# Routers with a place for every step's rows, three sets of moments, earlier masks, and an identity matrix that TensorE turns between its work

## The reference, cut to what matters

```python
x = x + 0.5 * _L0_ffn_ref(_layernorm(x), gate_w, w_gate, w_up, w_down)   # first router
x = x + _L0_attn_ref(_layernorm(x), ...)
x = x + 0.5 * _L0_ffn_ref(_layernorm(x), gate_w, w_gate, w_up, w_down)   # second router
...
# inside _L0_ffn_ref: T = 4096 tokens, E = 64 experts, K = 8, C = 128 places in an expert
logits = x2 @ gate_w.T
probs = softmax(logits)
top_w, top_i = top_k(probs, K)
pos = cumulative count of the token within its expert, over tokens in order
valid = pos < C
xg[e, pos] = x2[tok]                  # the experts' inputs
```

## Time and profile before

| | |
|---|---|
| median of 3 runs | 2716.4 us (2715.36 to 2718.21) |
| the profiled execution, its own time | 2715.87 us |
| its span in the profile | 2714.1 us |
| first router, from the first load to the table | about 7 to 105 us of the span |
| second router | about 1845 to 1944 us |
| mean granted clock of PE over the span | 0.948 |

### The profile page before, as it was taken

The page is one execution under the profiler, slowest core; times in us unless marked ns, Lnnn a source line. Parts: engine busy times, 40 slices in busy tenths (PEclk is TensorE's granted clock), DMA queues, the critical chain, the costliest instruction groups (busy, mean ns, idle before and its releaser), DMA issues. The chain is left out here.

```text
span 2714.1 us, 44233 instructions
## 1 busy us (share of the span) xinstructions
PE 2382.4 (88%) x16926; PEld 2110.7 (78%) x16926; DVE 1797.5 (66%) x3578; ACT 864.8 (32%) x1704; POOL 1239.9 (46%) x1214
## 2 busy tenths in 40 slices
PE   6556589999999999999999999986566488999998
PEld 6444479999999999999999999976454377888887
DVE  5433268888888888888888888865422256677654
ACT  4322233333333333333333333323322132333332
POOL 3378634555455455545554555452278622122111
PEclk9988799999999999999999999995599888999999
DMA  6999600000000000000000000004599710000000
GB/s 205 308 225 223 142 12 7 19 16 21 5 19 18 20 5 17 20 21 5 17 21 20 5 17 20 13 3 134 151 244 216 150 39 24 24 24 24 8 16 16
DMA packets 196928, 169.51 MB, mean 62 GB/s; under 512 B 28944, under 2 KB 189680, under 8 KB 196208
## 3 DMA queue, kind: packets, MB, share of 16 engines
q1 hardware_dynamic: 168144, 123.94, 15.5%
q0 software_dynamic: 24576, 37.77, 7.6%
q10 hardware_dynamic: 4000, 4.98, 0.6%
HBM read 117.94 MB, written 53.13 MB: 63 GB/s over the span
## 5 line engine op out<-in xcount | busy, mean ns | idle before, releaser
L971 POOL TENSOR_TENSOR a_orstd<-a_ms,minus_half 128x8 f32<-128x8 f32 x64 | 106.7, 1667 | 494.0 <-DVE a_ms L1131 494.0
L951 POOL TENSOR_SCALAR a_pick<-a_index,lut_row 128x258 f32<-128x258 int32 x240 | 280.7, 1170 | 24.3
L1124 DVE RECIPROCAL a_rz<-a_rz 128x256 f32<-128x256 f32 x128 | 215.5, 1715 | 0.0
L779 DVE TENSOR_TENSOR e_hT<-e_psH,e_sil 128x128 f32<-128x128 f32 x128 | 37.3, 291 | 259.6 <-ACT e_sil L737 259.6
L663 PE MATMUL e_psX<-ident,e_xg 128*128 128x128 f32 x256 | 61.6, 327 | 163.0 <-DMA e_xg<-rows,slot_tok 162.5
L663 PEld LDWEIGHTS e_psX<-ident,e_xg 128*128 128x128 f32 x256 | 30.6, 155 | 209.5 <-DMA e_xg<-rows,slot_tok 206.8
L1333 PEld LDWEIGHTS a_psD<-a_v,a_at 128*128 128x128 f32 x1536 | 181.3, 192 | 7.1 <-issue 1.4
L954 POOL TENSOR_TENSOR a_found<-a_found,a_pick 128x258 f32<-128x258 f32 x240 | 177.2, 738 | 20.0
L1333 PE MATMUL a_psD<-a_v,a_at 128*128 128x128 f32 x1536 | 181.9, 275 | 1.2 <-DVE a_at L1104 1.2
L633 POOL DMA_INDIRECT e_xg<-rows,slot_tok x128 | 127.4, 995 | 104.6 <-POOLq L252 66.2
L1104 DVE TENSOR_TENSOR a_at<-a_psB,causal 128x384 f32<-128x384 f32 x256 | 130.1, 550 | 49.2 <-PE a_psB L1270 49.2
(11 more groups left out here) (261 smaller groups left out, 7706.9 us busy)
## 6 DMA issues: line engine op xcount, KB each, us to landing
e_wg<-in_L_ffn_w_gate SPq DMA_DIRECT2D x128, 128.0 KB, 3.4
e_wu<-in_L_ffn_w_up SPq DMA_DIRECT2D x128, 128.0 KB, 3.7
e_wd<-in_L_ffn_w_down SPq DMA_DIRECT2D x128, 128.0 KB, 4.3
rows<-r_row SPq DMA_DIRECT2D x32, 320.0 KB, 3.2
stream_b<-r_zeros SPq DMA_DIRECT2D x11, 384.0 KB
stream_c<-rows SPq DMA_DIRECT2D x33, 128.0 KB, 3.3
r_xt<-in_L_attn_hidden_states SPq DMA_DIRECT2D x16, 256.0 KB, 3.8
stream_a<-r_xt SPq DMA_DIRECT2D x16, 256.0 KB, 4.4
```

The costliest lines, as they stand in the source:

```text
L951: nc.gpsimd.tensor_scalar(pick[:, :, :], index[:, :, :], float(c), w["lut"][:, c:c + 1], ALU.is_equal, ALU.mult).then_inc(picked, 1)
L971: nc.gpsimd.tensor_tensor(out=flat(orstd[:, :, :]), in0=ms[:, :], in1=cst["minus_half"][:, 0:TT * HQ], op=ALU.pow).then_inc(orstd_ok, 1)
L1124: nc.vector.reciprocal(rz[:, a, :], rz[:, a, :]).then_inc(rz_ok, 1)
```

## The change

What it does:

- `xt` and `row` get one place for each of the 8 steps. All loads are issued at the start, none waits, and `normalise` no longer waits for a written row. In the first router `keep` stands in the loop at every step.
- Moments, scale and shift get 3 places (S) in place of 2, and `moments_of` and `scales` run three steps ahead in place of two.
- On PE the masks of step j stand ahead of the scores of step j+1.
- PE transposes the identity matrix into a PSUM bank of its own, `psF`, that nobody reads (`occupy(n)`): 30 times ahead of the first turn and 10 behind it, and in a step 4 times behind the masks, 4 behind the scores and 12 behind the turn. The last two steps have fewer, so that a router has 172 in all.

```diff
-    R = 4
     NP = 4
+    S = 3
...
-        xt = mem.sb("xt", [P, R, 2, 2, D])
-        row = mem.sb("row", [P, R, 2, 2, ROW])
-        bs = mem.sb("bs", [P, 2, 4, 6])
+        xt = mem.sb("xt", [P, NJ, 2, 2, D])
+        row = mem.sb("row", [P, NJ, 2, 2, ROW])
+        bs = mem.sb("bs", [P, S, 4, 6])
...
+        psF = mem.ps("psF", [P, P])
...
                 def load(j):
-                    if j >= R:
-                        for u in range(2):
-                            sp.wait_ge(normed[u], 2 * (j - R) + 2)
-                        if fresh:
-                            sp.wait_ge(x_kept[j % R], 32 * (j // R))
                     for u in range(2):
-                        sp.dma_start(xt[:, j % R, u, :, :], xv[2 * j + u]).then_inc(x_here[j % R], 16)
+                        sp.dma_start(xt[:, j, u, :, :], xv[2 * j + u]).then_inc(x_here[j], 16)
...
-                for j in range(1, R):
+                for j in range(1, NJ):
                     load(j)
...
                 for j in range(NJ):
-                    if fresh and j < NJ - R:
+                    if fresh:
                         keep(j)
                     rows_written(j)
-                    if j + R < NJ:
-                        load(j + R)
...
-                    for j in range(NJ - R, NJ):
-                        keep(j)
...
                 def normalise(j):
                     act.wait_ge(shift_ok, j + 1)
-                    if j >= R:
-                        act.wait_ge(row_out[j % R], 32 * (j // R))
...
-                scales(0)
-                scales(1)
+                for j in range(S):
+                    scales(j)
                 for j in range(NJ):
-                    if j + 2 < NJ:
-                        scales(j + 2)
+                    if j + S < NJ:
+                        scales(j + S)
                     weigh(j)
...
-                moments_of(0)
-                moments_of(1)
+                for j in range(S):
+                    moments_of(j)
                 for j in range(NJ):
                     choose(j)
-                    if j + 2 < NJ:
-                        moments_of(j + 2)
+                    if j + S < NJ:
+                        moments_of(j + S)
...
+                def occupy(n):
+
+                    for k in range(n):
+                        nc.tensor.transpose(psF[:, :], cst["ident"][:, :], cst["ident"][:, :])
+
...
+                occupy(30)
                 turn(0)
+                occupy(10)
                 pe.wait_ge(gw_ready, 1)
                 score(0)
                 turn(1)
                 for j in range(NJ):
-                    if j + 1 < NJ:
-                        score(j + 1)
                     for u in range(2):
                         pe.wait_ge(chosen_ok[u], j + 1)
...
                                             cst["ident"][:, :]).then_inc(maskT[u], 1)
+                    if j + 1 < NJ:
+                        occupy(4)
+                        score(j + 1)
+                    occupy(4)
                     if j + 2 < NJ:
                         turn(j + 2)
+                        occupy(12)
```

More of the change, by code:

```diff
@@ L160, in moe_router @@
         zeros = mem.sb("zeros", [P, (NTOK // P + 1) * D // NZ]) if fresh else None
-        xt = mem.sb("xt", [P, R, 2, 2, D])
-        row = mem.sb("row", [P, R, 2, 2, ROW])
-        bs = mem.sb("bs", [P, 2, 4, 6])
[L164 to L168, removed]
+        xt = mem.sb("xt", [P, NJ, 2, 2, D])
+        row = mem.sb("row", [P, NJ, 2, 2, ROW])
+        bs = mem.sb("bs", [P, S, 4, 6])
+        mv = mem.sb("mv", [P, S, 4, 2])
+        ve = mem.sb("ve", [P, S, 4])
+        mean = mem.sb("mean", [P, S, 4])
+        rstd = mem.sb("rstd", [P, S, 4])
+        shift = mem.sb("shift", [P, S, 4])
         lnT = mem.sb("lnT", [P, 2, DC, 2 * P])
@@ L193, in moe_router @@
         psG = mem.ps("psG", [P, DC, E])
+        psF = mem.ps("psF", [P, P])
         gw_here, gw_turned, gw_ready = mem.sem("gw_here"), mem.sem("gw_turned"), mem.sem("gw_ready")
         zero_set, zero_out = mem.sem("zero_set"), mem.sem("zero_out")
-        x_here, x_kept, row_out = ([mem.sem(f"{n}{k}") for k in range(R)] for n in ("x_here", "x_kept", "row_out"))
+        x_here, x_kept, row_out = [mem.sem(f"x_here{k}") for k in range(NJ)], mem.sem("x_kept"), mem.sem("row_out")
         stats, moments, shifted, rstd_ok, shift_ok = (mem.sem(n) for n in ("stats", "moments", "shifted", "rstd_ok", "shift_ok"))
@@ L298, in _ @@
                         sp.dma_start(zv[:, k, :], zeros[:, :]).then_inc(zero_out, 16)
-                    for j in range(NJ - R, NJ):
-                        keep(j)
                     for raw, src, here in behind:
                         sp.dma_start(raw, src).then_inc(here, 16)
-                    for k in range(R):
-                        sp.wait_ge(x_kept[k], 32 * (NJ // R))
+                    sp.wait_ge(x_kept, 32 * NJ)
                     sp.wait_ge(zero_out, 16 * NZ + 32)
-                for k in range(R):
-                    sp.wait_ge(row_out[k], 32 * (NJ // R))
+                sp.wait_ge(row_out, 32 * NJ)
             @block.scalar
@@ L312, in normalise @@
                     act.wait_ge(shift_ok, j + 1)
-                    if j >= R:
-                        act.wait_ge(row_out[j % R], 32 * (j // R))
                     for u in range(2):
                         for h in range(2):
-                            nc.scalar.activation(row[:, j % R, u, h, 0:D], xt[:, j % R, u, h, :], ACT.Identity,
-                                                 bias=shift[:, j % 2, 2 * u + h:2 * u + h + 1],
-                                                 scale=rstd[:, j % 2, 2 * u + h:2 * u + h + 1]).then_inc(normed[u], 1)
+                            nc.scalar.activation(row[:, j, u, h, 0:D], xt[:, j, u, h, :], ACT.Identity,
+                                                 bias=shift[:, j % S, 2 * u + h:2 * u + h + 1],
+                                                 scale=rstd[:, j % S, 2 * u + h:2 * u + h + 1]).then_inc(normed[u], 1)
                 def turned_out(j):
@@ L382, in weigh @@
                     pool.wait_ge(rden_ok, j + 1)
-                    nc.gpsimd.tensor_tensor(out=row[:, j % R, :, :, :].rearrange("p u h c -> p (u h) c")[:, :, D:ROW], in0=ex[:, j % 2, :, :],
+                    nc.gpsimd.tensor_tensor(out=row[:, j, :, :, :].rearrange("p u h c -> p (u h) c")[:, :, D:ROW], in0=ex[:, j % 2, :, :],
                                             in1=rden[:, j % 2, :].unsqueeze(2).to_broadcast([P, 4, E]), op=ALU.mult).then_inc(weights, 1)
-                scales(0)
-                scales(1)
+                for j in range(S):
+                    scales(j)
                 for j in range(NJ):
-                    if j + 2 < NJ:
-                        scales(j + 2)
+                    if j + S < NJ:
+                        scales(j + S)
                     weigh(j)
@@ L497, in turn @@
                             for c in range(DC):
-                                nc.tensor.transpose(psT[u][:, c, h * P:(h + 1) * P], row[:, j % R, u, h, c * P:(c + 1) * P],
+                                nc.tensor.transpose(psT[u][:, c, h * P:(h + 1) * P], row[:, j, u, h, c * P:(c + 1) * P],
                                                     cst["ident"][:, :]).then_inc(turned[u], 1)
```

22 lines of the change are left out of this document (11 added, 11 removed).

## The result

| | before | after |
|---|---|---|
| median of 4 runs each | 2715.88 us (2710.7 to 2718.21) | 2699.64 us (2697.55 to 2703.7) |
| the profiled execution, own time / span | 2715.87 / 2714.1 us | 2703.7 / 2702.0 us |

The ratio is 0.9946, with a 95% interval of 0.9934 to 0.9957: 16.2 us less between the medians.

What follows compares the result with a forecast made beforehand. It took a ring of waits through PE, DVE, POOL and ACT at clock 0.50 to bound the routers, 6.96 us a step. 2 x (9.2 - 0.5) - 1.5 = 15.9 us less gave 2700.5 us, range 2694 to 2705.

Steps and rivals of the forecast that it cites:

- the sum: Whole kernel: 2 x (9.2 - 0.5) - 1.5 = 15.9 us less, giving 2700.5 us as the median.
- DVE sets the step: Router steps at clock 1.00: DVE's 5.6 us is longest; second to eighth choice takes 32.6 us in place of 41.77.
- choices farther apart than 5.6 us at a clock of 1.00: Router steps: a stated sign of being wrong; choices were expected 5.6 us apart.
- Does the clock rise?: Start of each router: PE's clock rises from 0.50 to 1.00 in the first 48 transposes and stays there.
- The masks ahead, the moments a step sooner. Both cut the ring.: Router steps: both reorderings leave a shorter ring, 5.1 us at clock 1.00 or 7.4 us at 0.50.
- the ring: Router loop of choice, moments, scales, normalising, turn, scores, masks, scans; two rounds make two steps, 41.77 us from second to eighth choice.
- The waits removed from `load` and `normalise` give nothing by themselves.: Router steps: no gain from removing these waits, as ACT waited for POOL's shift, not for a written row.
- The start: Each router up to its second choice: +0.5 us, with bounds of -2.0 to +1.1 us.
- The first router's DMA: First router's last counts: nearly full DMA could make them queue, +1.5 us, with bounds of 0 to about 10 us.
- The clock stays at 0.50: Rival, both routers: transposes don't raise the clock, a step takes 10.0 us, total about 2765 us; chance 0.18.
- The first router's queue: Rival: queued counts or traffic cost 6 to 10 us more, or the clock sometimes falls; 2705 to 2712 us; chance 0.14.
- No change: Rival: clock rises late, near the middle of each loop, so slow and fast steps cancel; 2711 to 2722 us; chance 0.05.

## Why the prediction was right, point by point

**The time.** Forecast 2700.5, measured 2699.64 us. Part of that exactness is luck: the routers of the profiled pair gave 11.1 us where the sum had 15.9, and its own time was 2703.7 where the forecast had 2700.0. The other three executions lie 2.7 to 6.2 us lower, and no trace shows where. The sign and the size of the main term are shown; the last 4 us are not.

**"DVE sets the step", 4 x 5.6 + 2 x 5.1 = 32.6 us.** Right in size: 32.9. It is made of four steps of 5.78 and two of 4.8 and 5.0. The 5.6 was DVE's work at 5.39 (too high by 0.2) without the 0.39 us beside POOL's L371, which the earlier trace rows could not show, as L371 and L404 did not meet there. One of the prediction's own signs of being wrong, choices farther apart than 5.6 us at a clock of 1.00, thus came true by this 0.2 us; it says that the size of DVE's step was off, not that another engine set it.

**"Does the clock rise?"** It rose among the first 30 transposes and stayed, as taken. With that the Trainium skill's rule, "TensorE: Matmul & The Clock Gate", "Part 4: PE-mode transpose", does not hold for these: nothing but transposes of 128 x 128 in fp32 ran on PE from 12.83 to 18.2 us and from 1844.56 to 1847.8 us, and the granted clock went from 0.50 to 1.00. (The durations beside the page's rule are for bf16.) "The step on which the sign hangs" holds only for a kernel with identities in it. The gain as a whole does not need the clock: places and moments alone give 0.9941, at a mean clock of 0.63 from 1858 to 1890 us.

**"The masks ahead, the moments a step sooner. Both cut the ring."** Half of this step failed. The moments cut it: taken back, the ring is 41 us again. The masks ahead don't: taken back, it is 0.5 us shorter, and the last choice another 0.65 us. They lengthen it, since the scores then wait for the choice. Without identities, with the clock at 0.50 or mostly so, this costs 4.2 to 4.9 us a router (36.56 against 32.39 and 31.65), and it is this wait that the identities then undo by the higher clock. One part of the change repairs what another breaks.

**"The waits removed from `load` and `normalise` give nothing by themselves."** True of the row that I read, ACT's wait for POOL, and wrong as a part of the sum: without the places, the rest of the change (moments three steps ahead, masks, identities) makes the kernel 1% slower than before. I costed the edit against the old order of work, not against the new one.

**The start, +0.5 us.** +1.1 and -0.6, within its bounds of -2.0 to +1.1. The turn of step 0 stands 5.28 us behind the gate's transposes, 3.48 before: the 2 us later that were to show it.

**"The first router's DMA", +1.5 us.** Mis-sized, and given to one router alone. The counts' way grew by 3.2 and 1.8 us. Of these the copies are 1.4. With the rows of the last steps moved too, the first router is 0.9 us under the way of before, and the second 0.5 us over it; the shorter steps put the same rows into less time. I had gone by the mean share (0.77), where what is under way at that moment decided. The share was to be near 1 throughout; it was 1.01 over the first 20 us and 0.82 in the steps.

**Not in the sum.** The last choice ends 0.6 us later in each router, because its two copies wait apart for their scores (0.61 and 0.53 us at 1891.63 and 1892.45 of the timeline). That too is the masks' new place, as it goes when they are put back.

**The rivals.** *The clock stays at 0.50* did not come; its price, a PE step of 10 us, shows in part in the kernel with identities in the old order (16 identities 3.62 us, steps of 9.4 to 10.7). *The first router's queue* came in small, and in both routers: 3.5 us beyond the sum's 1.5, where the rival had 6 to 10. *No change* did not.

## What to carry to other kernels

When a change has several parts, cost each against the order of work that the others make, and ask of every wait that is removed whether a part beside it would bring it back: here the change without the places is 1% slower than the kernel before, and places and a third set of moments alone give the whole gain. An engine kept busy for its clock pays only where its own speed is on the ring; first look whether an order on that engine put it there. Large transfers that nobody waits for yet are to be held back until a short one on the critical way has landed, and not only issued behind it; then look what comes next and now meets them.

## What the runs showed of the hardware that was not expected

- Transposes of the identity alone brought the granted clock from 0.50 to 1.00, twice in the change's trace, and with 20 of them a step it stayed there until 1895.5 us in the second router; with none in the steps it fell after 2 to 3 steps.
- Without any identity the clock rose by itself for some 7 us in the steps of two kernels (1861.4 to 1868.3 us with places and moments alone), where that of the kernel before stayed at 0.50 in its second router's steps.
- A DVE subtraction of 128 x 256 took 0.81 us in place of 0.42 beside a POOL multiplication of the same shape, and 0.43 inside a POOL power of 128 x 4 that itself is recorded with 1.04 us.
- The counts' transfer to DRAM took 7.6 us from issue to the next issue with rows and copies issued before and behind it, 4.3 without them. The first gather of the experts took 6.05 us from issue to PE where the DMA engines' share in the 2.7 us ahead of it was 1.05, and 3.72 where it was 0.00.
